# One fused attention and channel-mixing layer on one core: a new prologue and short steps, and the FFN's value product as three products of high and low parts

## What is computed

```python
a = layernorm(x)
q = a @ Wq + bq                              # 16 heads of 16
k, v = (a @ Wk + bk) @ Wc @ We, (a @ Wv + bv) @ Wc @ We    # 4 shared heads of 16
qf, kf = elu(q) + 1, elu(k) + 1
num = qf . cumsum(kf (x) v);  den = qf . cumsum(kf) + 1e-6      # over the tokens, causal
y = a + (num / den) @ Wo + bo
x2 = x + layernorm(y) * gamma + beta
z = layernorm(x2);  zp = z of the token before
xr, xk = mu_r * z + (1 - mu_r) * zp, mu_k * z + (1 - mu_k) * zp
out = x2 + sigmoid(xr @ W_r.T) * (relu(xk @ W_k.T) ** 2 @ W_v.T)
```

## Time and profile before

| | |
|---|---|
| median of 3 runs | 298.79 us |
| the profiled execution's own time | 300.61 us |
| its span in the profile | 298.8 us |
| busy PE / DVE / ACT / POOL | 272.9 / 235.1 / 145.4 / 128.8 us |
| share of PE in the chain that ended last | 76% |
| mean granted TensorE clock | 0.969 of full speed |

### The profile page before, as it was taken

The page is one execution under the profiler, slowest core; times in us unless marked ns, Lnnn a source line. Parts: engine busy times, 40 slices in busy tenths (PEclk is TensorE's granted clock), DMA queues, the critical chain, the costliest instruction groups (busy, mean ns, idle before and its releaser), DMA issues.

```text
span 298.8 us, 7425 instructions
## 1 busy us (share of the span) xinstructions
PE 272.9 (91%) x2923; PEld 192.7 (65%) x2923; DVE 235.1 (79%) x578; ACT 145.4 (49%) x294; POOL 128.8 (43%) x151
## 2 busy tenths in 40 slices
PE   7598798887899999999999999999999999977894
PEld 7565655745685578756885588557865677654663
DVE  6629569799799959996899779985999558989433
ACT  1238655545454756376455844484247520453540
POOL 2711660244474447436753567354344414063310
PEclk9789799997799999999999999999999999999999
DMA  6900202002000013000400020001100110002012
GB/s 175 274 12 3 72 1 72 2 3 70 3 2 0 2 37 105 2 3 3 140 2 0 2 73 0 2 2 35 37 5 0 37 37 2 0 0 71 35 37 70
DMA packets 12178, 10.73 MB, mean 36 GB/s; under 512 B 2288, under 2 KB 12144, under 8 KB 12144
## 3 DMA queue, kind: packets, MB, share of 16 engines
q1 hardware_dynamic: 11392, 9.97, 10.5%
q10 hardware_dynamic: 752, 0.30, 0.4%
HBM read 6.07 MB, written 4.19 MB: 34 GB/s over the span
## 4 chain that ended last, share of the span: by engine, by line
PE 76%; DVE 10%; ACT 5%; issue 3%; DMA 2%; ACTq 1%; POOL 1%; DVEq 0%
PE ps_x L448 9%; PE ps_x L478 8%; PE ps_x L370 7%; PE ps_x L463 6%; PE ps_z L419 6%; PE ps_x L470 6%; PE ps_y L440 5%; PE ps_x L364 5%; PE ps_y L435 5%; PE ps_z L470 4%; PE ps_x L456 2%; PE ps_z L463 2%; PE ps_x L357 2%; DVE probs L953 2%; PE ps_z L402 2%
## 5 line engine op out<-in xcount | busy, mean ns | idle before, releaser
L953 DVE TENSOR_TENSOR probs<-ps_z,causal 128x512 f32<-128x512 f32 x64 | 40.8, 679 | 6.7 <-PE ps_z L419 6.7
L273 POOL TENSOR_TENSOR out_tok<-tanh_r,x_tok 128x512 f32<-128x512 f32 x14 | 18.7, 1338 | 27.7 <-DVE tanh_r L1026 27.7
L1026 DVE SCALAR_TENSOR_TENSOR tanh_r<-tanh_r,ps_x 128x512 f32<-128x512 f32 x13 | 8.9, 687 | 27.0 <-PE ps_x L478 27.0
L448 PE MATMUL ps_x<-wo_sb,oT 128*128 128x256 f32 x128 | 29.6, 382 | 0.0
L250 POOL TENSOR_TENSOR xb_tok<-x_in,beta_bc 128x1024 f32<-128x1024 f32 x8 | 18.9, 2361 | 24.8 <-DVE x_tok L999 24.8
L370 PE MATMUL ps_x<-aT,wq_sb 128*128 128x512 f32 x60 | 27.8, 604 | 0.0
L478 PE MATMUL ps_x<-wvT,k_act 128*128 128x256 f32 x104 | 25.6, 389 | 1.0 <-ACT k_act L773 1.0
L243 POOL TENSOR_TENSOR abo_tok<-a_tok,bo_bc 128x1024 f32<-128x1024 f32 x8 | 18.9, 2360 | 17.3 <-issue 12.6
L217 POOL TENSOR_TENSOR neg_mean<-mv,neg_one 128x4 f32<-128x4 f32 x16 | 5.0, 311 | 49.4 <-DVE mv L884 49.4
L448 PEld LDWEIGHTS ps_x<-wo_sb,oT 128*128 128x128 f32 x128 | 23.6, 190 | 3.8 <-issue 0.9
L213 POOL TENSOR_TENSOR rstd<-rstd,neg_half 128x4 f32<-128x4 f32 x24 | 24.9, 1037 | 1.9
(11 more groups left out here) (133 smaller groups left out, 584.2 us busy)
## 6 DMA issues: line engine op xcount, KB each, us to landing
x_in<-in_L_attn_x_dram SPq DMA_DIRECT2D x8, 512.0 KB, 4.3
out_dram<-out_tok SPq DMA_DIRECT2D x16, 256.0 KB, 2.1
xr<-in_L_attn_Wq_dram ACTq DMA_DIRECT2D x1, 256.0 KB, 4.0
xk<-in_L_ffn_W_r_dram SPq DMA_DIRECT2D x1, 256.0 KB, 5.4
xk<-in_L_ffn_W_k_dram SPq DMA_DIRECT2D x1, 256.0 KB, 5.7
xr<-in_L_ffn_W_v_dram SPq DMA_DIRECT2D x1, 256.0 KB, 7.2
wo_sb<-in_L_attn_Wo_dram SPq DMA_DIRECT2D x4, 64.0 KB, 4.8
bo_bc<-in_L_attn_bo_dram SPq DMA_DIRECT2D x1, 128.0 KB, 5.5
```

What stands on the lines that cost most here:

```text
L448: last = mm(bk_[:, (b % 2) * D:(b % 2 + 1) * D], oT[m % 2][:, a, b, :], wo_sb[:, a, :], start=(a == 0), stop=(a == 1))
L953: V.tensor_tensor(probs[b % 2][:, 2 * h:2 * h + 2, :].rearrange("p g (r s) -> p g r s", s=HALF), ps_z[:, 2 * h:2 * h + 2, 0:2 * P].rearran ...
```

## The change

Four things change.

1. **Prologue.** ACT copies the folded weights as they come, then a transposed, and only then Wq. DVE makes the bias operand and scales a of chunk 0 without waiting for `q_in`. POOL puts the causal mask's memset and all behind it after `s_a >= 4`. One pair of PE's `keep_busy` products goes.
2. **Short steps.** In steps 0 and 1 DVE follows `short_step`: in step 1 the key features come before centre, the second residual after the last mask, and the second statistics after `divide(c, 2)`. POOL does the denominators' product and the second norm first there, and adds bo and beta afterwards. In all steps ACT's second copy of a transposed comes after the spread reciprocals; in step 0 PE's first weight transposes come after scores(0, 1).
3. **Value product.** In the full steps `mix_v` becomes `mix_v_parts`: k_act and W_v are each split in a high part, rounded to float32r by a copy on ACT, and a low part, the difference. The product is high x high + high x low + low x high, 6 products of 128x256 for each 128 tokens in place of 2. ACT gains two copies a step, DVE two subtractions (`low_part`); W_v is split once, in step 0, by ACT and POOL. In the finale `mix_v` stays as it was.
4. **Order in the full steps.** PE does the denominators and outputs(c, 3) ahead of both halves of the value product. DVE does `key_sums` ahead of `second_stats`, the reciprocal and `divide(c, 3)` ahead of both gates; POOL does `prod` ahead of the second norm.

The diff, cut to its core:

```diff
+        ka_p, wv_p = ([ctx.enter_context(nc.sbuf_tensor(f"{name}_{part}", [P, *shape], F32R)) for part in ("high", "low")]
+                      for name, shape in (("ka", (2, T)), ("wv", (KD, D))))
...
@@ POOL, step @@
-                if c == 0:
-                    pool.wait_ge(s_kf, 2 * n + 2)
-                add_bo(n)
-                add_beta(n)
                 if f >= 0:
-                    second_norm(m)
-                    denominator_terms(n)
-                elif m >= 0:
+                    add_bo(n)
+                    add_beta(n)
                     denominator_terms(n)
                     second_norm(m)
+                else:
+                    if m >= 0:
+                        denominator_terms(n)
+                        second_norm(m)
+                    else:
+                        pool.wait_ge(s_kf, 2 * n + 2)
+                    add_bo(n)
+                    add_beta(n)
+                    if m < 0:
+                        pool.wait_ge(wv_split, 1)
+                        PL.tensor_tensor(wv_p[1][:], wvT[:], wv_p[0][:].bitcast(F32), ALU.subtract).then_inc(wv_split, 1)
...
             norm_x(0)
+            pool.wait_ge(s_a, 4)
             link(PL.memset(causal[:], 1.0))
@@ PE @@
+            def mix_v_parts(m, i, bk_):
+                pe.wait_ge(s_kah, 2 * m + 2)
+                for b in (2 * i, 2 * i + 1):
+                    out = bk_[:, (b % 2) * D:(b % 2 + 1) * D]
+                    for k in range(KD):
+                        for part in range(2):
+                            mm(out, ka_p[0][:, k, b * P:(b + 1) * P], wv_p[part][:, k, :], start=(k == 0 and part == 0), stop=False)
+                    if b == 0:
+                        pe.wait_ge(s_kal, 2 * m + 2)
+                    for k in range(KD):
+                        last = mm(out, ka_p[1][:, k, b * P:(b + 1) * P], wv_p[0][:, k, :], start=False, stop=(k == KD - 1))
+                last.then_inc(s_v_ps, 1)
...
                 outputs(c, 2)
                 if f >= 0:
-                    mix_v(f, 0, x1)
                     pe.wait_ge(s_rl, 2 * f + 2)
...
                 denominators(n)
                 outputs(c, 3)
                 if f >= 0:
+                    pe.wait_ge(wv_split, 2)
+                    mix_v_parts(f, 0, x1)
                     pe.wait_ge(s_kT, 2 * n + 2)
-                    mix_v(f, 1, x2)
+                    mix_v_parts(f, 1, x2)
                 scores(n, 0)
...
@@ ACT @@
                 AC.activation(k_act[:, n, :], k_act[:, n, :], ACT.Square).then_inc(s_ka, 1)
+                if parts:
+                    act.wait_ge(s_ka, 2 * m + n + 1)
+                    copy(ka_p[0][:, n, :], k_act[:, n, :]).then_inc(s_kah, 1)
...
-                a_out(n)
+                a_out(n, 0)
                 reciprocals(c)
+                a_out(n, 1)
...
+                    act.wait_ge(ffn_w_sb, 3)
+                    copy(flat(wv_p[0]), flat(wvT)).then_inc(wv_split, 1)
...
-            act.wait_ge(dve_const, 1)
+            act.wait_ge(dve_const, 2)
@@ DVE @@
+            def low_part(m, n):
+                dve.wait_ge(s_kah, 2 * m + n + 1)
+                if m >= 1:
+                    dve.wait_ge(s_v_ps, 2 * m)
+                V.tensor_tensor(ka_p[1][:, n, :], k_act[:, n, :], ka_p[0][:, n, :].bitcast(F32), ALU.subtract).then_inc(s_kal, 1)
...
-            dve.wait_ge(q_in, Q_IN)
-            V.tensor_scalar(neg_bq[:], bq_col[:], -1.0, None, ALU.mult)
-            V.tensor_scalar(bq_1[:], bq_col[:], 1.0, None, ALU.add).then_inc(dve_const, 1)
+            dve.wait_ge(bias_in, BIAS_IN)
+            dve.wait_ge(dve_const, 1)
+            for i in range(2):
+                last = V.tensor_scalar(bkv_lhs[0:64, i, :], ones[0:64, :], bkv_col[0:64, i:i + 1], None, ALU.mult)
+            last.then_inc(bias_lhs, 1)
...
             norm_x(1)
+            dve.wait_ge(q_in, Q_IN)
+            V.tensor_scalar(neg_bq[:], bq_col[:], -1.0, None, ALU.mult)
+            V.tensor_scalar(bq_1[:], bq_col[:], 1.0, None, ALU.add).then_inc(dve_const, 1)
             dve.wait_ge(prep_sb, 3)
```

More of the change, by code:

```diff
@@ L11 @@
 F32 = mybir.dt.float32
+F32R = mybir.dt.float32r
 AX_X = mybir.AxisListType.X
@@ L506, in step @@
                     out_projection(m, 1, x2)
-                else:
+                scores(c, 1)
+                if m < 0:
                     pe.wait_ge(ffn_w_in, FFN_IN)
@@ L510, in step @@
                     ffn_weight(0, x1)
-                scores(c, 1)
                 keys_values(n)
@@ L684, in copy, with a_out @@
                 return AC.activation(dst, src, ACT.Copy, **kw)
[L686 removed]
+            def a_out(n, k):
                 if n >= 1:
                     act.wait_ge(s_q_ps, 2 * n)
[L689 to L691 removed]
+                act.wait_ge(s_aT_ps, 2 * n + k + 1)
+                copy(aT[:, k, :], (x2, x0)[k][:, :]).then_inc(s_aT, 1)
             def keys(n):
@@ L841, in _ @@
                     act.dma_start(dst, src).then_inc(q_in, 16)
+            act.wait_ge(prep_ps, 1)
+            copy(wcT[0:64, :], z0[0:64, 0:64])
+            copy(wkvT[0:64, :, :].rearrange("p i n -> p (i n)"), z1[0:64, :]).then_inc(prep_sb, 1)
+            act.wait_ge(prep_ps, 2)
+            copy(cewe[0:64, :], z0[0:64, 128:128 + KV]).then_inc(prep_sb, 1)
+            act.wait_ge(prep_ps, 3)
+            copy(flat(wkv_sb), ps_y[:, 0:256])
+            copy(bkv_bc[:], ps_y[:, 256:384]).then_inc(prep_sb, 1)
+            a_out(0, 0)
+            a_out(0, 1)
             act.wait_ge(q_in, Q_IN)
@@ L1035, in step, with short_step @@
                     norm_x(n + 1)
-                if f >= 0:
-                    token_shift(f, 0, *for_r)
-                    token_shift(f, 1, *for_r)
+                if f < 0:
+                    short_step(c, n, m)
+                    return
+                token_shift(f, 0, *for_r)
+                token_shift(f, 1, *for_r)
+                add_residual(m, 0, x1)
+                add_residual(m, 1, x2)
+                mask(c, 1)
+                keys_values(n)
+                centre(m)
+                key_features(n)
+                second_residual(m)
+                divide(c, 0)
+                mask(c, 2)
+                queries(n, 0, x0)
+                token_shift(f, 0, *for_k)
+                token_shift(f, 1, *for_k)
+                queries(n, 1, x1)
+                divide(c, 1)
+                states(n)
+                key_sums(n)
+                second_stats(m)
+                mask(c, 3)
+                divide(c, 2)
+                low_part(f, 0)
+                low_part(f, 1)
+                reciprocal(n)
+                divide(c, 3)
+                gate(f, 0, x1)
+                gate(f, 1, x2)
+            def low_part(m, n):
[3 more added lines that the diff above has]
+                V.tensor_tensor(ka_p[1][:, n, :], k_act[:, n, :], ka_p[0][:, n, :].bitcast(F32), ALU.subtract).then_inc(s_kal, 1)
+            def short_step(c, n, m):
                 if m >= 0:
@@ L1051, in step @@
                 queries(n, 0, x0)
-                if f >= 0:
-                    token_shift(f, 0, *for_k)
-                    token_shift(f, 1, *for_k)
+                if m >= 0:
+                    centre(m)
                 queries(n, 1, x1)
@@ L1139, in _ @@
             norm_x_scale(0)
-            dve.wait_ge(bias_in, BIAS_IN)
-            dve.wait_ge(dve_const, 2)
-            for i in range(2):
-                last = V.tensor_scalar(bkv_lhs[0:64, i, :], ones[0:64, :], bkv_col[0:64, i:i + 1], None, ALU.mult)
-            last.then_inc(bias_lhs, 1)
             norm_x(1)
+            dve.wait_ge(q_in, Q_IN)
+            V.tensor_scalar(neg_bq[:], bq_col[:], -1.0, None, ALU.mult)
+            V.tensor_scalar(bq_1[:], bq_col[:], 1.0, None, ALU.add).then_inc(dve_const, 1)
             dve.wait_ge(prep_sb, 3)
```

48 lines of the change are left out of this document (13 added, 35 removed).

## The result

The changed kernel takes **289.52 us** (median of 4 runs, 289.32 to 291.18), the kernel before 298.74 in the same comparison: a ratio of 0.970, 95% interval 0.965 to 0.975. The forecast was 288.6 in a range of 285.5 to 296.0. The profiled execution took 289.32 us, its span is 287.6 at a mean granted clock of 0.982. All ratios and ranges of this document leave out three executions of the kernel before, of 355, 445 and 653 us.

A forecast was written before the change was run, and what follows sets the result against it. PE was taken to bound the five full steps (busy 31.59 of 31.80 us), DVE next. Prologue -5.9, step 0 -0.9, steps 1 and 2 +2.0, full steps -5.4: -10.2 from 298.8, 288.6 us; range 285.5 to 296.0.

The forecast's parts named there:

- Prologue, -5.9: Before the first keys and values: ACT no longer waits for Wq, so L364 starts at 12.4 for 18.32.
- The clock that I expected to stay at full: Prologue: with PE's wait cut from 3.02 to some 0.4, the clock stays at 2.4 GHz, 2.5 us less.
- Step 0, -0.9: Step 0: scores come 1.6 us sooner, part is given back, and the queries come 0.9 sooner.
- Steps 1 and 2, +2.0: Short steps: POOL's two additions delay `dz`, hence DVE's second queries and PE's `mix_k`, by 2.0 us.
- late `z_tok`: End of step 1: `z_tok` starts 1.4 later, so PE starts step 2 0.7 us late.
- 4 us or more: Sign in step 2: `dz` starts at least this long after the `z_tok` chain's nbias.
- one of the bounds: Steps 1 and 2: +3.5 if PE's new idle stretch before step 2 also halves its clock for a while.
- Value product, 3.86 to 2.98: Full steps: 24 float32r products at 124 ns replace two float32 calls, 0.88 us less a step.
- Rival 1: Value product: float32r at float32's pace, 216 ns a product, 1.32 us more a step, 300.6 us; chance 0.12.
- rival 2: Value product: no limit by weight loads, 108 ns a product, 1.27 us less a step, 287.6 us; chance 0.15.
- The stall of 0.20: Full steps: PE's wait before `mix_v` goes, since denominators and outputs(c, 3) stand there, 0.20 us a step.
- The covers: Full steps: other engines' results are ready 0.5 to 1 us before PE needs them, so PE does not stall.

The follow-up runs named there:

- number 5: The changed kernel run again, unaltered, beside the kernel before: 290.01 us, ratio 0.968.
- number 10: The kernel before with 20 more filler transposes on PE ahead of its first prologue wait for ACT's copies: 296.51 us, ratio 0.986.
- numbers 1: The kernel before with the changed prologue alone: 293.11 us, ratio 0.977.
- 2: The changed kernel with the old prologue and the old orders of the short steps: 295.35 us, ratio 0.985.
- numbers 7: The changed kernel with 20 unread filler products in PE's three idle stretches of step 1: 290.20 us, ratio 0.969.
- 6: The changed kernel with POOL's addition of beta for chunk 2 moved behind `dz` of step 2: 291.89 us, ratio 0.973.
- number 12: The changed kernel with the old order on POOL alone in the short steps, DVE's new order kept: 292.12 us, ratio 0.970.
- number 3: The changed kernel with DVE's and POOL's old order in steps 0 and 1: 287.43 us, ratio 0.960.
- number 11: The changed kernel with DVE's and POOL's old short-step order, and the three-part value product also in the finale: 287.38 us, ratio 0.956.
- 8: The changed kernel with both step 1 filler products on PE and beta's addition for chunk 2 behind `dz`: 290.52 us, ratio 0.969.
- number 9: The changed kernel with the fourth product, low x low, added in the full steps: 294.58 us, ratio 0.979.
- number 4: The changed kernel with the value product in float32 at its new place, without high and low parts: 293.19 us, ratio 0.978.

## Why the prediction was right

**Prologue, -5.9: right in kind, 0.7 short in the profiled execution.** L375 starts at 11.74 for 12.4, the clock is 1.00 from 8 to 16. PE reaches its second stage at 7.33, where I had 8.0: its transposes of the weights and the filler behind them ran at full clock (0.63 and 0.61, 1.06 and 0.80 before), and ACT's copies ended at 7.28. That is the clock of this execution and not the change: in number 5, the same program, the transposes take 1.06 again, the second stage starts at 7.81, and L375 at 12.73. The clock that I expected to stay at full did so in nine of eleven profiled executions of the new prologue, and fell to 0.50 in two; 5.4 to 6.7 us is what the eleven gained up to L375, against the 18.32 of before. What I had not priced is what the clock is worth outside the prologue: number 10.

**Step 0, -0.9 for -1.6: too small, and more than half of the gain has another reason.** The step takes 1.59 less. Before, it held 3.0 us at a clock of 0.52 (31 to 34 us); without that, but with the old order, it takes 21.41 to 21.48 (numbers 1, 2 and 10), 0.9 less, and the order gives another 0.7. I had put all 0.9 on the order. In three executions of kernels with the new order of ACT and PE the step was 22.35, 23.34 and 22.34 (numbers 7, 6 and 12), each with half clock in it: from 24 to 32 us the mean is 0.79, 0.57 and 0.79.

**Steps 1 and 2, +2.0: the mechanism named is there, the closeness of the sum is in part chance.** `mix_k` comes 2.1 us later from step 1's mark than before (48.90 for 46.80; 1.7 in number 5), for the 2.0 forecast. But that is two things. Against the old order in the same kernel (number 3) the new one costs more, 2.4 in number 5 and 2.8 in the profiled execution; and the old order itself is 0.7 shorter than in the kernel before, which had more of step 1 at half clock (a mean of 0.88 over the step, 0.94 in number 3). From number 3 against number 5, both with one stretch at half clock late in step 1: step 1 is 1.2 longer (forecast 0.7, for a late `z_tok`; 0.9 against number 11, the same order as number 3), step 2 is 1.15 (1.3, for queries that make `mix_k` late). Numbers 7 and 8 have step 1 at full clock and take the same 28.29. `dz` starts 4.6 us behind nbias, for "4 us or more"; `mix_k` waits 0.93 us for DVE where the clock is full, and number 12 ties that wait to the two additions. One thing was missed: in the profiled execution PE ran at 0.51 in place of that wait, which was one of the bounds and not the forecast. Removing either delay brings up the other (numbers 6 to 8).

**Value product, 3.86 to 2.98: 3.06 measured, with some luck.** The pace is 0.120 us a product and 0.127 with the changes at the block's ends. I took 0.124 from products of 128 columns, as 1.98 / 16. That is an average too, which holds one change of 0.213: in the trace the other starts of that row are 0.112 apart. Read rightly, it gives 24 x 0.112 + 0.2 = 2.89, and 3.06 is more than that, since the products of parts came 0.008 us slower each than the row's; no run shows why. So the row was the nearest, but it is no exact measure of this product. Rival 1 (216 ns) and rival 2 (108 ns) are both out. (Rival 1 says that it decides from 222 ns on; by its own terms the kernel is 1.5 us slower from 213 on.) Beside it the Trainium skill (TensorE: Matmul & The Clock Gate, LDWEIGHTS) has a load of 128 columns at 107 ns; the 112 of the float32 products of 128 columns is near it, the 120 of the parts is not. The Trainium skill's other page (FP8 and Floating Point Precision, TensorE Precision Notes), by which float32 is four passes, agrees with number 9: as one block, four products of parts cost 4.01 us where float32 costs 3.66 (number 4), and three cost 3.06, a sixth less.

**The stall of 0.20: right, but the order gives 0.43.** The forecast set the block of parts against two float32 calls, 3.86, and so counted under the parts what comes from joining two blocks into one. Number 4 tells them apart: the stall 0.20 and the joining 0.20 belong to the order, and the parts give 0.60, not 0.88. The two sum to 1.02 for the forecast's 1.08: the sum of a step is right, its division is not.

**The covers held**: low parts ready 0.58 us before their reader (forecast 0.5), `prod` 0.42 (0.6), DVE 29.20 busy (29.4). The full step is PE's own work, as number 9 shows: what is added to PE lands whole in the step.

The sum came out 0.9 low against the median. The terms by the spans are -6.6 - 1.6 + 2.1 - 5.1 = -11.2, for a forecast of -10.2. The median moved by only 9.2, since the profiled execution of before lies 1.9 above its median and that of after on its own; in number 5, with more executions, it moved by 10.7. The forecast lies between the two. Such differences go with the clock: single executions of the kernel before spread from 297.5 to 302.8 us, the shortest at a mean granted clock of 0.985, the longest at 0.966.

## What to carry to other kernels

Where TensorE is busy for all of a step, price an edit by PE's own time alone: what number 9 added to PE came back whole. Read the pace from the starts inside a row and the changes at its ends apart from it, and compare one block with one block; here 1.98 / 16 and 2 x 1.93 mixed the two, and the errors happened to be small. An operation that is moved ahead on one engine moves others back; before keeping such an order, look at what the next step waits for: here the denominators came 1.8 us sooner and the step ended 1.2 us later. One profiled execution is not enough to read a prologue: the same program started its keys and values at 11.74 in one and at 12.73 in another. And an order on two engines that share a buffer is one decision: putting back one half of it made steps 1 and 2 take 62.5 us, where they take 60.2 with the new order and 57.9 with the old.
